# Pairing the value products of a batch, and another order for the first stretch, in a fused transformer block on one core

## The reference

```python
def _tc_rmsnorm(x, t, gw, gb, bw, bb):
    g = (t @ gw.T + gb)[:, None, :]
    b = (t @ bw.T + bb)[:, None, :]
    inv_rms = jax.lax.rsqrt(jnp.mean(x * x, axis=-1, keepdims=True) + EPS)
    return g * x * inv_rms + b
def _attention(x, Wq, Wk, Wv, Wo):          # 16 heads of 8 features
    attn = jnp.einsum('blhd,bmhd->bhlm', q, k) / scale
    p = jax.nn.softmax(attn, axis=-1)
    o = jnp.einsum('bhlm,bmhd->blhd', p, v).reshape(B, L, D)
    return o @ Wo.T
def _swiglu(x, gate_w, hid_w, out_w):       # 512 hidden features
    return jax.nn.silu(x @ gate_w.T) * (x @ hid_w.T) @ out_w.T
h = x + _attention(_tc_rmsnorm(x, ...first norm...), Wq, Wk, Wv, Wo)
y = h + _swiglu(_tc_rmsnorm(h, ...second norm...), gate_w, hid_w, out_w)
out = x + y
```

## Time and profile before

| | |
|---|---|
| median of 3 runs | 257.89 us (257.65 to 258.99) |
| profiled execution | 257.42 us, span 255.6 us |
| TensorE busy / weight loads | 221.2 us (87%) / 177.9 us (70%) |
| VectorE, ScalarE, GpSimd busy | 202.9, 163.3, 111.9 us |
| mean granted TensorE clock | 0.963 |
| beat 0 begins | 32.83 us |

### The profile page before, as it was taken

One profiled execution on the slowest core, in us unless ns is written; L12 is line 12 of the kernel. 1 busy time (PEld: TensorE's weight loads), 2 busy tenths in 40 slices (PEclk: granted clock), 3 DMA queues, 4 the chain that ended last, 5 costly groups with the idle time before them and its releaser, 6 DMA issues.

```text
span 255.6 us, 8235 instructions
## 1 busy us (share of the span) xinstructions
PE 221.2 (87%) x3048; PEld 177.9 (70%) x3048; DVE 202.9 (79%) x490; ACT 163.3 (64%) x352; POOL 111.9 (44%) x183
## 2 busy tenths in 40 slices
PE   2436777879989999899989999999999999899894
PEld 2314545547667868786878877887888778687894
DVE  4646966897899889889988998899888997565673
ACT  5354658676876686669766777567757655666430
POOL 8323852597265254625381516252623232323320
PEclk9995579999999999999999999999999999999998
DMA  5866601530261026100540045004500000000001
GB/s 162 345 169 147 185 4 28 152 85 3 64 166 27 26 64 164 47 23 19 140 124 0 27 112 152 10 27 114 156 6 26 4 26 3 23 3 24 22 21 44
DMA packets 18819, 18.79 MB, mean 74 GB/s; under 512 B 3644, under 2 KB 17980, under 8 KB 18652
## 3 DMA queue, kind: packets, MB, share of 16 engines
q1 hardware_dynamic: 18252, 17.80, 24.7%
q10 hardware_dynamic: 528, 0.46, 0.8%
HBM read 3.22 MB, written 2.10 MB: 21 GB/s over the span
## 4 chain that ended last, share of the span: by engine, by line
PE 45%; issue 24%; POOL 16%; DVE 9%; ACT 4%; ACTq 1%; POOLq 0%; DVEq 0%
PE proj L489 7%; PE pv L427 6%; PE ffn L320 5%; PE ffn L322 3%; PE ffn L321 3%; PE score L410 3%; DVE nmax L756 3%; POOL inv L923 3%; PE raw L383 3%; POOL qp L915 2%; PE tok L442 2%; POOL xn_lo L936 2%; POOL kp L915 2%; POOL xs L929 2%; PE proj L349 2%
## 5 line engine op out<-in xcount | busy, mean ns | idle before, releaser
L756 DVE TENSOR_REDUCE nmax<-raw 128x8 f32<-128x1024 f32 x61 | 74.2, 1216 | 3.0 <-PE raw L383 2.9
L597 ACT ACTIVATE p_s<-score 128x1024 f32<-128x1024 f32 x64 | 65.5, 1023 | 16.1 <-PE score L410 14.9
L427 PE MATMUL pv<-p_s,va 128*32 128x128 f32 x1024 | 41.7, 280 | 1.8 <-ACT xn L615 1.1
L320 PE MATMUL ffn<-xn_hi,ffn_hi 128*128 128x256 f32 x106 | 34.8, 328 | 1.2 <-POOL xn_lo L936 1.2
L626 ACT ACTIVATE th<-ffn 128x256 f32<-128x256 f32 x53 | 20.3, 384 | 19.6 <-PE ffn L322 19.6
L489 PE MATMUL proj<-ffn_out_s,hT 128*128 128x128 f32 x240 | 31.6, 275 | 0.0
L813 DVE SCALAR_TENSOR_TENSOR gated<-th,ffn 128x256 f32<-128x256 f32 x53 | 22.0, 415 | 12.1 <-ACT th L626 11.7
L427 PEld LDWEIGHTS pv<-p_s,va 128*32 128x32 f32 x1024 | 24.7, 109 | 9.2 <-issue 4.0
L936 POOL TENSOR_TENSOR xn_lo<-xn,xn_hi 128x128 fp32r<-128x128 f32 x32 | 14.7, 460 | 34.6 <-DVE xn_hi L804 34.6
L322 PE MATMUL ffn<-xn_hi,ffn_lo 128*128 128x256 f32 x106 | 29.7, 280 | 0.0
L321 PE MATMUL ffn<-xn_lo,ffn_hi 128*128 128x256 f32 x106 | 29.6, 279 | 0.0
(11 more groups left out here) (130 smaller groups left out, 456.0 us busy)
## 6 DMA issues: line engine op xcount, KB each, us to landing
ks<-kp SPq DMA_DIRECT2D x48, 128.0 KB, 2.4
qs<-qp SPq DMA_DIRECT2D x45, 128.0 KB, 2.5
out_y<-x_s SPq DMA_DIRECT2D x16, 128.0 KB, 1.8
x_s<-in_x SPq DMA_DIRECT2D x1, 1536.0 KB, 10.9
qs<-shift SPq DMA_DIRECT2D x64, 4.0 KB
x_s<-in_x SPq DMA_DIRECT2D x2, 256.0 KB, 3.6
ffn_in_s<-in_ffn_in_w SPq DMA_DIRECT2D x1, 512.0 KB, 6.7
qs<-qp ACTq DMA_DIRECT2D x3, 128.0 KB, 3.7
```

The source lines that it names most:

```text
L320: pe.matmul(dst, w_hi, v_hi, start=True, stop=False)
L427: mm = pe.matmul(pv[VW * j:VW * j + VW, (t % 2) * L:(t % 2 + 1) * L], va[vbuf(g)][:, t // 2, at:at + VW], p_s[:, (BEATS * g + t) % PBUF, p ...
L597: act.activation(p_s[:, n % PBUF, :], score[:], ACT.Exp, scale=SCALE).then_inc(s_exp, 1)
L756: dve.tensor_reduce(heads[:, :, t % 2, :], raw_dst(g, t)[:].rearrange("l (e j m) -> l e j m", e=HALVES, j=HQ), AX.X, ALU.max, negate=True) ...
```

## The change

The value products of a batch (two halves) are issued together in even beats, at beat 8g + 2 + 2i, just after the raw scores; odd beats have none. In odd beats V, query, y and the transpose `c_tro` stand between the raw scores and the FFN matmuls, and maximum transpose, XT1 and `c_wo` behind them. In even beats the order behind the FFN is `c_tr2`, y, `d_xt2`, key. Up to beat 9 `c_tr2` moves one beat later, behind the score. ScalarE's copy of V moves ahead of the tanh. In the first stretch the first key is made in two halves; GpSimd makes the low weights before the second power; ScalarE does the norms of group 1 before it issues three DMAs; the FFN weights are split there; maxima and transposes interleave otherwise; V of group 0 moves to beat 0, V of group 1 from beat 1 to beat 6, and the raw scores of beats 0 and 1 are others.

```diff
-    PV = 1
+    VALUE_1 = 6
-            return score if g == 0 and t % 2 and t < BEATS - 1 else raw
+            return score if g == 0 and t % 2 and t < HQ else raw
...
+        def raws_in(T):
+            if T < 2:
+                return [(0, BEATS - 2 + T)]
+            return due(T, RAW, BEATS)
...
-                elif g == 1:
-                    pe.wait_ge(s_va, 1)
                 else:
-                    pe.wait_ge(s_qrest, g + 1)
+                    pe.wait_ge(s_qrest, max(g + 1, 3))
...
+            def first_key():
+                pe.wait_ge(s_wlo, 1)
+                for n in range(2):
+                    half = slice(2 * n * L, 2 * (n + 1) * L)
+                    pe.wait_ge(s_lo1, n + 1)
+                    mm = split_product(key_dst(0)[:, half], qk_hi[:, 1, :], qk_lo[:, 1, :], xn1_hi[:, half],
+                                       xn1_lo[:, half])
+                mm.then_inc(s_k, 1)
...
                 if g == 0 and t == 0:
-                    pe.wait_ge(s_max, BEATS - 2)
+                    pe.wait_ge(s_max, HQ)
...
                 for g, t in due(T, 0, BEATS):
                     c_score(g, t)
-                for g, t in due(T, RAW, BEATS):
+                for g, i in due(T - 1, TR2, NB, 2):
+                    if T - 1 < FFN:
+                        c_tr2(g, i)
+                if T == 0:
+                    a_values(0)
+                for g, t in raws_in(T):
                     b_raw(g, t)
-                for g, t in due(T, PV, BEATS):
-                    c_pv(g, t, T)
-                for g, i in due(T, TRO, NB, 2):
-                    c_tro(g, i)
+                for g, i in due(T, OT, NB, 2):
+                    c_pv(g, 2 * i, T)
+                    c_pv(g, 2 * i + 1, T)
+                if T % 2:
+                    for g, _ in due(T, VALUE, since=2):
+                        a_values(g)
+                    for g, _ in due(T, QUERY, since=2):
+                        a_query(g)
+                    for w in range(WIN):
+                        for g, half in due(T, OUT + WSTEP * w, 2):
+                            d_out(g, w, half)
+                    for g, i in due(T, TRO, NB, 2):
+                        c_tro(g, i)
                 for g, p in due(T, FFN, PIECES):
                     d_gate_up(g, p)
-...
+                if T % 2:
+                    for g, half in due(T, MAXT, 2, HQ):
+                        b_maxT(g, half, T)
+                    if T == 1:
+                        b_raw(1, 0)
+                    for g, b in due(T, XT1, NB, 2, since=3):
+                        a_transpose(g, b, T)
+                    for g, i in due(T, WO, NB, 2):
+                        c_wo(g, i)
+                else:
+                    for g, i in due(T, TR2, NB, 2):
+                        if T >= FFN:
+                            c_tr2(g, i)
+                    for w in range(WIN):
+                        for g, half in due(T, OUT + WSTEP * w, 2):
+                            d_out(g, w, half)
+                    for g, i in due(T, XT2, NB, 2):
+                        d_xt2(g, i, T)
+                    if T == VALUE_1:
+                        a_values(1)
+                    for g, _ in due(T, KEY, since=2):
+                        a_key(g)
...
             a_middle(0, s_qrest, q_rest, qp, s_qmid)
-            stack_high_queries()
             a_norm(1, 2)
             a_norm(1, 3)
+            stack_high_queries()
...
                 for g, i in due(T, TRO, NB, 2):
                     c_oT(g, i)
+                for g, _ in due(T, VALUE, since=2):
+                    a_values(g)
                 for g, p in due(T, FFN, PIECES):
                     d_tanh(g, p)
```

More of the change, by code:

```diff
@@ L386, in b_raw, with b_maxT @@
                 mm.then_inc(s_raw, 1)
-            def b_maxT(g, half):
+            def b_maxT(g, half, T):
                 pe.wait_ge(s_max, BEATS * g + HQ * (half + 1))
+                for f, i in due(T - 1, XT2, NB, 2):
+                    pe.wait_ge(s_xn2, NB * f + i + 1)
                 if g == 0 and half == 0:
@@ L418, in c_pv @@
                 pe.wait_ge(s_exp, BEATS * g + t + 1)
-                for f, i in due(T - 1, XT2, NB, 2):
+                for f, i in due(T - 2, XT2, NB, 2):
                     pe.wait_ge(s_xn2, NB * f + i + 1)
@@ L501, in _ @@
                 a_transpose(0, b)
-            a_key(0)
+            first_key()
             a_query(0)
@@ L530, in _ @@
                 for g, p in due(T, FFN, PIECES):
                     d_gate_up(g, p)
-                for g, half in due(T, MAXT, 2, HQ):
-                    b_maxT(g, half)
-                for g, b in due(T, XT1, NB, 2, since=3):
-                    a_transpose(g, b, T)
-                for w in range(WIN):
-                    for g, half in due(T, OUT + WSTEP * w, 2):
-                        d_out(g, w, half)
-                for g, i in due(T, WO, NB, 2):
-                    c_wo(g, i)
@@ L541, in _ @@
-                for g, i in due(T, XT2, NB, 2):
-                    d_xt2(g, i, T)
-                for g, i in due(T, TR2, NB, 2):
-                    c_tr2(g, i)
-                for g, _ in due(T, VALUE, since=1):
-                    a_values(g)
-                for g, _ in due(T, KEY, since=2):
-                    a_key(g)
-                for g, _ in due(T, QUERY, since=2):
-                    a_query(g)
+                if T % 2:
[20 more added lines that the diff above has]
+                        a_key(g)
@@ L668, in _ @@
             a_middle(1, s_krest, k_rest, kp, s_kmid)
+            a_mean(2)
+            zero_fill(va[1][:].rearrange("l b v -> l (b v)"), s_va0[1])
             a_middle(1, s_qrest, q_rest, qp, s_qmid)
-            a_mean(2)
             a_mean(3)
-            zero_fill(va[1][:].rearrange("l b v -> l (b v)"), s_va0[1])
-            a_norm(2, 0)
-            a_norm(2, 1)
-            a_values(0)
-            a_norm(2, 2)
-            a_norm(2, 3)
+            for b in range(NB):
+                a_norm(2, b)
             for T in range(LAST + 1):
@@ L851, in _ @@
             a_hi(1, 1)
+            dve.wait_ge(s_ffnin, 16)
+            dve.tensor_copy(ffn_hi[:], ffn_in_s[:]).then_inc(s_whi, 1)
             zero_values(0)
             a_rest(1, key_dst(1), kp, k_rest, s_khi, s_klo, s_krest)
+            b_max(0, 0)
+            b_max(0, 1)
             a_rest(1, query_dst(1), qp, q_rest, s_qhi, s_qlo, s_qrest)
-            for t in range(HQ):
-                b_max(0, t)
+            b_max(0, 2)
+            b_max(0, 3)
             b_shift(0, 0)
-            for t in range(HQ, BEATS - 1):
-                b_max(0, t)
+            b_max(0, 4)
+            b_max(0, 5)
             for T in range(LAST + 1):
@@ L978, in _ @@
             a_lo(1, 1)
+            pool.wait_ge(s_whi, 2)
+            pool.tensor_tensor(ffn_lo[:], ffn_in_s[:], ffn_hi[:].bitcast(F32), ALU.subtract).then_inc(s_wlo, 1)
             a_lowest(1, k_rest, kp, s_kmid, s_klo)
+            a_inv(2)
+            a_scale(2)
             a_lowest(1, q_rest, qp, s_qmid, s_qlo)
             surround_values(0)
-            a_inv(2)
-            a_scale(2)
             a_inv(3)
```

24 lines of the change are left out of this document (8 added, 16 removed).

## The result

The changed kernel takes 273.39 us in the median of four runs (273.07 to 273.56), and the kernel before, on the same chip, 257.78: a ratio of 1.0587 (95% interval 1.056 to 1.0614), slower by 15.6 us. The profiled execution took 273.34 us with a span of 271.4. The forecast was 263.5 with a range of 256.5 to 267.0: the direction was right, and the loss is 2.6 times the one foretold and lies outside the range. Of all executions behind the times of this document, one of e8 (259.76 us) and one of the kernel before (307.8 us) fell into a slower state of the chip and are left out.

A forecast was written before the change was run, and what follows sets the result against it. TensorE was taken to bound the steady part, most of its waits covered by blocks of some 0.9 us. Stretches +8.3, start -1.0 and end -1.2 made +6.1 on 257.42: 263.5 us, range 256.5 to 267.0.

The forecast's parts named there:

- I take -1.0 at beat 8, between +0.5 and -3: First stretch and first beats: earlier start, partly eaten by serial maxima and late key 2, brings beat 8 1.0 us earlier.
- Beat 0 at 31.6: Start: the first score, before at 32.83, comes at 31.6, with 1.2 us estimated for the DMA queue and maxima.
- From beat 8 ... +1.4: Stretch of eight beats from beat 8: new losses at XT1, query and `c_tro`, less removed waits and pair savings: +1.4 us.
- the rival of the clock: TensorE's standstills in six beats each bring a lower-clock spell costing 1.0 us: 269.5 us in all; chance 0.07.
- 29.6; that is +2.3, and I take +2.2: Stretch from beat 16: 27.32 us becomes 29.6, taken as +2.2 because waits overlap; same for beats 24 to 31.
- That saves 0.14 us for each pair of beats, 0.55 for a stretch: Paired value products: the second adds 0.44 us where it cost 0.58, saving 0.55 us in eight beats.
- 1.5 for the query: Early query in odd beats: TensorE waits about 1.5 us for the key's remainder to free `proj`; bounds 0.7 and 1.7.
- XT1's price: Odd beats 11 to 39: the score after the first-norm transpose loses 0.50 us each, 2.0 us a stretch.
- Beats 40 to 55 ... +0.3: Beats without XT1: new query, V and `c_tro` waits, less removed waits and pair savings: +0.3 us.
- -1.2, between -2.5 and +0.3: From beat 56 to the end: four pairs save 0.55 us and `c_tr2` ahead of y covers the longest wait: -1.2 us.
- cover without cost: ScalarE finishes the first norm in time, so scores after XT1 in odd beats 11 to 39 don't wait: 256.5 us; chance 0.16.
- half of it: Query waits only 0.7 us and XT1 0.3: 257.5 to 258.5 us, no difference to be told; chance 0.09.

The follow-up runs named there:

- e8: Kernel before, with GpSimd's powers of a later group first, ScalarE's second norm ahead of the means, `c_tro` behind the FFN in beats 8g+7: 256.04 us.
- e7: Kernel before with the changed first stretch, plus eleven matmuls in beat 1 that nothing reads: 259.02 us, ratio 1.0031.
- e5: Changed kernel with the first stretch put back as it was before: 272.80 us, ratio 1.0565.
- e2: Changed kernel with the query alone put back at the end of its odd beat: 270.59 us, ratio 1.0481.
- e3: Changed kernel with V and y put back behind the first-norm transpose, query still early: 272.02 us, ratio 1.0538.
- e1: Changed kernel with V, query and y of odd beats put back behind the first-norm transpose: 268.70 us, ratio 1.0418.
- e12: Changed kernel with V, query and y late, and `c_tro` behind the FFN in all odd beats: 266.21 us, ratio 1.0320.
- e14: Changed kernel with XT1 ahead of the FFN, ScalarE's first norm ahead of the tanh, and the query late: 269.12 us, ratio 1.0418.
- e13: Changed kernel with XT1 ahead of the FFN and ScalarE's first norm ahead of the tanh: 268.41 us, ratio 1.0386.
- e6: Changed kernel with one value product a beat again instead of pairs: 272.36 us, ratio 1.0553.
- e11: Kernel before with the three moves of e8, and the FFN weight split moved into the first stretch: 254.94 us, ratio 0.9886.

## Why the prediction was wrong

The mechanisms foretold are in the profile one by one; the sum is 9.7 us short of the spans. It is short by 3.5 at beat 8, 1.5 in beats 8 to 15, 1.0 in 16 to 39, 1.2 in 40 to 55, and 2.5 at the end.

*"I take -1.0 at beat 8, between +0.5 and -3"*: this step failed most, at +2.5. "Beat 0 at 31.6" was nearly right (31.19). The prediction named the serial maxima, and took -1.0 without a sum; V of group 0 in beat 0, V of group 1 in beat 6 and the lower clock have no price in it. Beat by beat against before, from 0 to 7: +0.93 (V of group 0), +0.41, +1.40, +0.47, -0.75, +0.46, +1.04 (V of group 1 in beat 6), +0.15, less the 1.64. The 1.40 of beat 2 is mostly the half clock (its pair takes 1.93 us, 1.08 later), of which the prediction had the row and weighed it only for the later waits; e7 shows that in the old beats the longer spell costs 2.2 us by beat 8. In the changed beats the old first stretch is no cure (e5: beat 8 at 56.97), since there V of group 1 stands in beat 1 ahead of the maximum's transpose, and the pairs come at the lower clock as well (beat 2 is 3.72 us long, 3.01 before).

*"From beat 8 ... +1.4"*: +2.93. The query's wait in beat 11 was 1.67, against 1.5. Then beat 11 is 0.66 us longer than beat 19, which waits 1.61, and beat 12 is 0.45 longer than the beat 12 of e2: the clock fell there, 1.1 us. This is the rival of the clock, with the price foretold (1 us), but once and not six times: beats 19 and 27 wait 1.61 and keep 1.00. It is no accident of one execution. The profiles of e3 and e5 have the same 1.67 us in beat 11 and the same slow FFN (beats of 5.85 and 5.75 us), and e1, e2, e12 and e14, whose query is late, have neither. But e13 has the 1.67 us as well, and its beat 11 takes 4.35 us with matmuls at full speed. So the wait belongs to the fall and is not enough for it; what else it takes was not tried.

*"29.6; that is +2.3, and I take +2.2"*: 29.77, +2.45, and 28.89 against 28.5 from beat 32. The terms, by the idle time of their rows: pair 1.01 us against 1.02 (0.58 and four quads more, 0.44), query 1.61 against 1.5, V 0.52 against 0.44, low part in beat 22 0.24 against 0.3, and `c_tro` in beats 13 and 51 0.99 and 1.00 against 1.0. XT1's four places show 0.43, 0.53, 0.43 and 0.54 at the next score; the row behind the forecast's 0.50 shows 0.43, so the longer ones, which have no maximum's transpose ahead, are 0.1 above it. So the sum was right here, but not as a set of causes. "That saves 0.14 us for each pair of beats, 0.55 for a stretch" is true of the pair's own time and false of the kernel up to beat 40: e6, without pairs, has a stretch from 16 of 29.21, 0.56 shorter, since one product in the odd beat covers the wait for V and part of the query's, and leaves the low part of beat 22 time. And 1.5 for the query is true of the wait and false as a price: e2 got back 0.66 a stretch for it. XT1's price stands as a sum (e13: 1.59 of 2.0), not place by place.

*"Beats 40 to 55 ... +0.3"*: +1.5. V's 0.52 and 1.00 at `c_tro` are there; besides, the key of beat 42 starts some 0.3 us late, as GpSimd's low part ends, the raw scores of beats 47 and 55 come 0.45 us after their score where 0.23 is usual, and beat 43 waits 1.05 at the query where 0.95 was given.

*"-1.2, between -2.5 and +0.3"*: +1.3, the third failure. The sum had a pair's saving and a covered wait; instead `c_tro` waits 0.33 in beat 57 and 1.22 in beat 59, where it has neither raw scores nor y ahead. Before, the value products of beats 58 and 59 waited 0.23 and 0.26 and `c_tro` in beat 59 0.32. And in the last beats y now waits for the window before it:

```profile
261.76 1.13 PE L503 MATMUL proj<-ffn_out_s,hT 128*128 128x128 f32 x8 [1.03 <-DVE x_s L854]
```

e1, which has y late in odd beats, ends 24.3 us after its beat 63 and the changed kernel 24.7; the rest of this part, most of its 2.5 us, was not taken apart, and its cause stays open.

Of the rivals, *cover without cost* is excluded by the score's waits, *half of it* by the stretch from 16.

## What to carry to other kernels

Before moving an operation away, list for each operation behind it in the same queue how long after its producer it would now come: the time of a block between producer and consumer is cover, and two moves that each bare one place need not add up (8.3 and 12.0 us gave 13.0). A wait is worth its length only if nothing behind it ends at the same producer; follow the producer's queue (here means, norm, rounding, exponential on ScalarE) for the length of the beat before pricing the waits. Here a start 1.7 us earlier was worth nothing, since the next beats are serial, and their gaps cost the clock as well.

## What the runs showed of the hardware

- A wait of 1.67 us on TensorE in beat 11 is followed by 3.2 us at a mean clock of 0.64; e3 and e5 show the same. Waits of 1.61 us in beats 19 and 27 are followed by no fall. That beats 8 and 9 have no FFN does not explain it, for the same holds in e13, where beat 11 keeps 1.00:

```profile
73.18 0.50 PE L326 MATMUL proj<-xn_hi,qk_hi 128*128 128x512 f32 x1 [1.67 <-DVE k_rest L758]
```

- The clock's record can be missing early on: V of group 0 at 31.73 took 1.90 us for eight matmuls, and 1.13 at 91.38, while the record has no fall before 36.7. The profile of e13 says 1.00 throughout, with a pair of 1.93 us at 40.43 and another at 50.29. Durations of a known block are the safer reading; they bear out e7's 1.00 (its beat 2 takes 2.85 us, against 3.01 in the kernel before).
- A 128x128 VectorE operation with two inputs from SBUF took 2.11 us beside a GpSimd one of 2.35 us, and 0.29 us in e11 in the same beat, where GpSimd had done its work earlier. It ends 0.14 us after GpSimd's operation (53.59 against 53.45). The kernel before has such a meeting too, with a cast of one input, which takes 0.24 us in e11:

```profile
52.43 2.36 POOL L1006 TENSOR_TENSOR ffn_lo<-ffn_in_s,ffn_hi 128x1024 fp32r<-128x1024 f32 x1
53.62 1.26 DVE L804 CAST xn_hi<-xn 128x128 fp32r<-128x128 f32 x1
```

It ends 0.09 us after GpSimd's operation. So in both meetings the VectorE operation lasts until just after GpSimd's is done. The Trainium skill (GPSIMD Engine Reference, section 1, Specifications) says that the two engines share their SBUF interfaces and contend where VectorE has two SBUF inputs or is in a 2-port perf mode, without a size; the row of e8 agrees, and whether the cast was in such a mode no run here shows.
- Two value products in a row take 1.01 us from their start to that of the next block, and one 0.58, so the second adds 0.43.
